# Attention over user histories: the softmax of a superblock two units earlier

## The reference

```python
cand = candidate_features @ Wi + bi                       # 512 x 64
hist = history_features @ Wi + bi                         # 512 x 200 x 64
hidden = relu((cand @ Wq)[:, None, :] + hist @ Wk)
scores = where(seq < history_length, hidden @ Wv, -1e9)   # 512 x 200
attn = softmax(scores, axis=1)
interest = einsum('bs,bse->be', attn, hist)
avg = sum(hist * mask, axis=1) / history_length
x = concatenate([interest, cand, avg], axis=1)
x = relu(bn(x @ W1 + b1)); x = relu(bn(x @ W2 + b2)); x = relu(bn(x @ W3 + b3))
return sigmoid(x @ Wo + bo)
```

## Time and profile before

| | |
|---|---|
| median of 3 runs | 216.58 us (216.19 to 216.93) |
| profiled execution, its own time | 215.18 us |
| its span, first to last instruction | 213.2 us |
| TensorE busy | 202.0 us, 95% |
| VectorE busy | 175.0 us, 82% |
| ScalarE busy | 103.6 us, 49% |
| GpSimd busy | 62.5 us, 29% |
| granted TensorE clock, mean | 0.989 |

### The profile page before, as it was taken

The page is one execution under the profiler, slowest core; times in us unless marked ns, Lnnn a source line. Parts: engine busy times, 40 slices in busy tenths (PEclk is TensorE's granted clock), DMA queues, the critical chain, the costliest instruction groups (busy, mean ns, idle before and its releaser), DMA issues.

```text
span 213.2 us, 6305 instructions
## 1 busy us (share of the span) xinstructions
PE 202.0 (95%) x2123; PEld 81.7 (38%) x2123; DVE 175.0 (82%) x1087; ACT 103.6 (49%) x302; POOL 62.5 (29%) x112
## 2 busy tenths in 40 slices
PE   7999999999999999999999999999999998996583
PEld 3433324343434334343434343434434343433321
DVE  1458464989989898989898998989798989989990
ACT  2045365636365553636463636556364646265423
POOL 7903041231506060504223150606051320504000
PEclk9999999999999999999999999999999999999995
DMA  6999999797969797988979797879798890000000
GB/s 188 408 425 415 413 411 363 237 323 242 329 241 334 236 324 246 307 291 293 311 241 329 235 313 270 313 223 311 263 315 298 252 340 29 3 0 3 5 0 0
DMA packets 10225, 53.72 MB, mean 252 GB/s; under 512 B 1105, under 2 KB 2001, under 8 KB 10194
## 3 DMA queue, kind: packets, MB, share of 16 engines
q1 hardware_dynamic: 9906, 52.95, 70.1%
q10 hardware_dynamic: 288, 0.37, 0.6%
HBM read 53.32 MB, written 0.00 MB: 250 GB/s over the span
## 4 chain that ended last, share of the span: by engine, by line
PE 85%; DVE 9%; issue 3%; ACT 1%; POOL 1%; POOLq 0%; DVEq 0%; ACTq 0%
PE hist_ps L397 42%; PE key_ps L412 23%; PE score_ps L423 11%; DVE scratch L553 5%; PE attn_ps L441 5%; PE score_ps L367 3%; DVE kept L540 2%; DVE attended L553 1%; ACT result L335 0%; POOLq L61 0%; PE attn_ps L480 0%; PE attn_ps L379 0%; POOL rest L265 0%; DVE scores L562 0%; DVE average L573 0%
## 5 line engine op out<-in xcount | busy, mean ns | idle before, releaser
L307 ACT ACTIVATE hidden<-key_ps,query 128x200 f32<-128x200 f32 x252 | 87.2, 429 | 88.5 <-PE key_ps L412 88.5
L540 DVE SCALAR_TENSOR_TENSOR kept<-item,lens,hist_ps 128x200 f32<-128x200 f32 x256 | 93.5, 415 | 11.5 <-PE hist_ps L397 11.5
L397 PE MATMUL hist_ps<-history,params 128*64 128x400 f32 x512 | 100.5, 512 | 0.7 <-DVE kept L540 0.7
L553 DVE CUSTOM_DVE_ANT_0 scratch<-attn_ps,kept 128x200 f32<-128x200 f32 x236 | 71.9, 359 | 16.0 <-PE attn_ps L441 16.0
L412 PE MATMUL key_ps<-kept,params 64*64 64x400 f32 x504 | 57.1, 521 | 0.6 <-DVE kept L540 0.2
L397 PEld LDWEIGHTS hist_ps<-history,params 128*64 128x64 f32 x512 | 30.6, 136 | 40.7 <-issue 26.9
L260 POOL TENSOR_SCALAR attn<-weights,inv_sum 128x200 f32<-128x200 f32 x15 | 6.5, 434 | 118.3 <-DVE inv_sum L568 118.3
L412 PEld LDWEIGHTS key_ps<-kept,params 64*64 64x64 f32 x504 | 13.5, 131 | 35.7 <-issue 27.0
L423 PE MATMUL score_ps<-hidden,wv_rows 128*32 128x200 f32 x512 | 25.0, 336 | 0.1
L441 PEld LDWEIGHTS attn_ps<-parts,spread 64*64 64x64 bf16 x472 | 14.8, 107 | 26.4 <-issue 16.5
L441 PE MATMUL attn_ps<-parts,spread 64*64 64x200 bf16 x472 | 21.1, 247 | 3.4 <-DVE parts L640 2.2
(11 more groups left out here) (70 smaller groups left out, 59.4 us busy)
## 6 DMA issues: line engine op xcount, KB each, us to landing
history<-history_dram SPq DMA_DIRECT2D x63, 800.0 KB, 4.9
history<-history_dram SPq DMA_DIRECT2D x2, 400.0 KB, 4.9
candT<-candidates_dram SPq DMA_DIRECT2D x1, 256.0 KB, 5.6
params<-parameters_dram SPq DMA_DIRECT2D x1, 248.5 KB, 12.4
params<-parameters_dram ACTq DMA_DIRECT2D x1, 226.5 KB, 2.6
lens_raw<-lengths_dram ACTq DMA_DIRECT2D x1, 136.0 KB, 4.0
probability<-result SPq DMA_DIRECT2D x1, 2.0 KB
```

The lines of the kernel that those rows point to most:

```text
L307: act.activation(hidden[:, g % HID_SLOTS, v, :], banks[:, v, at * SEQ:(at + 1) * SEQ], ACT.Relu, bias=query[:, 2 * g + v:2 * g + v + 1]).t ...
L397: product = pe.matmul(hist_ps[64 * h:64 * h + 64, g % 2, 0:QCOLS], param("wi"), history[:, slot, h, 2 * at:2 * at + 2, :].rearrange("f p s ...
L540: dve.scalar_tensor_tensor(out=kept[:, g % KEPT_SLOTS, u, :], in0=item[:, :], scalar=pair_len[:, col:col + 1], in1=hist_ps[:, g % 2, u * S ...
L553: dve.tensor_tensor_reduce(scratch[:, at, v, :], banks[:, at, v * SEQ:(v + 1) * SEQ], kept[:, q % KEPT_SLOTS, v, :], 1.0, 0.0, ALU.mult, A ...
```

## The change

`DELAY` goes from 9 to 7. The maximum of a superblock moves into the unit of its score (4j + 5, behind that unit's masked sums), the exponential ahead of the relus of unit 4j + 4 (those whose keys follow the score on TensorE), the reciprocal to the start of unit 4j + 6. The boundary of the MLP's two parts moves from unit 56 to unit 58, and with it the mean of the first part from unit 58 to unit 60. Behind the loop seven units are left for nine; the last score is made in two halves, the first ahead of the keys of unit 63, the second after two spreads; there are six warm-up matmuls for three, and the first two MLP stages come ahead of them. The last split on VectorE has four steps for five: the first two are fused into one for part a, and the rest is made by one instruction from weights, reciprocal and part a. The sums of unit 59 no longer stand between its steps.

```diff
-DELAY = 9
+DELAY = 7
 SCORE_AT = SB_UNITS + 1
-MAX_AT = SCORE_AT + 1
-TAIL_WARMUPS = 3
+TAIL_WARMUPS = 6
-PART_UNITS = UNITS - 8
+PART_UNITS = UNITS - 6
...
             for unit in range(UNITS):
-                j, at = divmod(unit + 1 - MAX_AT, SB_UNITS)
-                relu(unit)
+                j, at = divmod(unit + 1 - SCORE_AT, SB_UNITS)
                 if at == 0 and j >= 0:
                     exponent(j)
+                relu(unit)
             exponent(LAST)
...
-            def score(j):
-                pe.wait_ge(relu_done, 2 * SB_QUADS * (j + 1))
+            def score(j, steps=range(SB_UNITS)):
+                pe.wait_ge(relu_done, 2 * SB_QUADS * j + UNIT_PAIRS * steps.stop)
 
                 wait(pe, max_ready, j - 1)
-                for k in range(4):
+                for k in steps:
                     for c in range(4):
...
-                product.then_inc(scored, 1)
+                if steps.stop == SB_UNITS:
+                    product.then_inc(scored, 1)
...
             first = UNITS - DELAY
+            score(LAST, range(0, 2))
             keys(UNITS - 1)
             spread_attn(first)
             spread_attn(first + 1)
+            score(LAST, range(2, SB_UNITS))
             spread_attn(first + 2)
+            mlp_stage(0, 0)
+            mlp_stage(0, 1)
 
             pe.wait_ge(max_ready, LAST)
             for _ in range(TAIL_WARMUPS):
                 keep_busy((LAST + 1) % 2)
-            score(LAST)
             spread_attn(first + 3)
             spread_attn(first + 4)
-            mlp_stage(0, 0)
-            mlp_stage(0, 1)
+            mlp_stage(0, 2)
             spread_attn(first + 5)
+            mlp_stage(0, 3)
             spread_attn(first + 6)
-            mlp_stage(0, 2)
-            spread_attn(first + 7)
-            mlp_stage(0, 3)
-            spread_attn(first + 8)
             mlp_stage(1, 0)
...
             for unit in range(UNITS):
-                masked_sum(2 * unit)
-                j, at = divmod(unit - MAX_AT - 1, SB_UNITS)
+                j, at = divmod(unit - SCORE_AT - 1, SB_UNITS)
                 if at == 0 and j >= 0:
                     invert(j)
+                masked_sum(2 * unit)
                 masked_sum(2 * unit + 1)
-                j, at = divmod(unit - MAX_AT, SB_UNITS)
+                j, at = divmod(unit - SCORE_AT, SB_UNITS)
                 if at == 0 and j >= 0:
                     maximum(j)
...
             attended_sum(first)
-            attended_sum(first + 1)
             store_interest(0)
             mean(1)
+            attended_sum(first + 1)
+            maximum(LAST)
             attended_sum(first + 2)
-            maximum(LAST)
-            attended_sum(first + 3)
             invert(LAST)
...
-            dve.tensor_scalar(attn[:, :], weights[:, bank, :], inverse, None, ALU.mult).then_inc(split_steps, 1)
             dve.tensor_scalar(part_a[:, :], weights[:, bank, :], inverse, param("keep1"),
                               ALU.mult, ALU.mult).then_inc(split_steps, 1)
-            attended_sum(first + 4, (0,))
+            dve.wait_ge(split_steps, done + 1)
+            dve.scalar_tensor_tensor(out=rest[:, :], in0=weights[:, bank, :], scalar=inverse, in1=part_a[:, :],
+                                     op0=ALU.mult, op1=ALU.subtract).then_inc(split_steps, 1)
             dve.wait_ge(split_steps, done + 2)
-            dve.tensor_tensor(rest[:, :], attn[:, :], part_a[:, :], ALU.subtract).then_inc(split_steps, 1)
-            attended_sum(first + 4, (1,))
+            dve.tensor_scalar(part_b[:, :], rest[:, :], param("keep2"), None, ALU.mult).then_inc(split_steps, 1)
             dve.wait_ge(split_steps, done + 3)
-            dve.tensor_scalar(part_b[:, :], rest[:, :], param("keep2"), None, ALU.mult).then_inc(split_steps, 1)
-            attended_sum(first + 4, (2,))
-            dve.wait_ge(split_steps, done + 4)
             dve.wait_ge(attn_spread, SB_UNITS * (LAST - 1))
             dve.tensor_tensor(parts[:, bank, :], rest[:, :], part_b[:, :], ALU.subtract).then_inc(parts_ready, 1)
-            attended_sum(first + 4, (3,))
-            for unit in range(first + 5, UNITS):
+            for unit in range(first + 3, UNITS):
                 attended_sum(unit)
             store_interest(1)
```

## The result

The changed kernel takes **211.69 us** in the median of 6 runs (211.09 to 212.40), the kernel before, in the same session, 216.8 (216.19 to 217.76): ratio 0.977, interval 0.9744 to 0.9795. That is 5.1 us less; 2.3 less and at best 213.3 were forecast. The sign held; the gain is about twice what the sum gave, and the time lies outside the range.

A forecast was written before the change was run, and what follows sets the result against it. TensorE was taken to bound the loop (85% of the chain), VectorE's sums and the last parts the end. Terms 0.1 - 0.84 + 0.75 - 0.3 - 2.05 = -2.3 us, from 216.58 to 214.3; range 213.3 to 216.1.

The forecast's parts named there:

- late relus: ScalarE, score's unit: relus behind the exponential start 0.05 us late in each of fifteen superblocks, +0.75 us (0.15 to 2.25).
- From there the work is the same: sixteen sums, interest, four layers: Behind the spread of the last parts: remaining work unchanged, so no gain or loss beyond the -2.05 us before it.
- I put the difference on the median: Whole kernel: profiled execution 215.18 us, median 216.58; the 1.40 between them was carried over to the changed kernel's time.
- The three added fillers fall into TensorE's wait: End of kernel: added warm-up matmuls fall into TensorE's 2.17 us wait for the last parts' spread; no time effect was counted.
- the late bound: ScalarE, score's unit: if nothing overlaps the exponential's accumulator read, relus are 0.15 us late per superblock, 2.25 in all.
- the rivals that need 0.20 or more: Loop, ScalarE: relu's wait of 0.20 us per superblock, 216.5, chance 0.09; exponential binding from 0.21, 218.7, chance 0.08.
- VectorE's lateness: Loop, fourth unit: late masked sum stalls TensorE's projection 0.07 us; moving the maximum removes it twelve times, -0.84 us.
- The mean in unit 60: Before superblock 14's maximum: exponential, relus and keys 0.5 us late once, against 0.79 saved at the old place, -0.3 us.
- The end: From the loop's last spread to the last parts' spread: reciprocal 1.36 us earlier, shorter split, -2.05 us in all.
- the rival by which the end gains 0.7: Behind the loop: another late input leaves half the reciprocal's gain and none in the split; whole -1.0, 215.6 us, chance 0.13.
- The parts: Loop, GpSimd: parts ready before the first spread needing them, cover 0.28 us after release, cost nothing.
- The rival with late parts: Loop, GpSimd: parts 0.5 us later miss their spread, 0.22 lost per superblock, whole +1.0, 217.6 us, chance 0.03.

The follow-up runs named there:

- moved_gap: Kernel before with maximum, exponential and reciprocal moved, delay 9 and old end kept, plus ten warm-up matmuls in the wait for the last parts: median 213.84 us.
- after_more: Kernel after with twelve warm-up matmuls for six in the wait for the last parts and one more on each side of spread 62: median 211.68 us.
- moved_only: Kernel before with only maximum, exponential and reciprocal moved, delay 9 and the old end kept: median 216.1 us, ratio 0.9918.

## Why the prediction was wrong in size

Stages of the profiles, us, from the timelines; "usual before" is the second profile of the kernel before:

| stage | usual before | after | difference | forecast |
|---|---|---|---|---|
| start to first score | 21.72 | 21.30 | -0.42 | 0 |
| first superblock | 11.36 | 11.47 | +0.11 | +0.1 |
| second score to the loop's last spread | 158.50 | 157.36 | -1.14 | -0.44 |
| to the spread of the last parts | 10.48 | 8.65 | -1.83 | -2.05 |
| to the output's DMA | 10.94 | 9.34 | -1.60 | 0 |

The sum is -4.9, and the spans are 214.6 and 209.7. (The loop's forecast is -0.84, -0.3 and 14 of the 15 late relus, +0.70.)

**The step that failed** is "From there the work is the same: sixteen sums, interest, four layers", together with "I put the difference on the median". The work is the same, but in most executions of the kernel before it ran at half the clock, from about 2 us after the 2.17 us wait. The profile on which the sum was made is of the rare executions in which the clock falls only at 208.5. The 1.40 by which it lay under the median were this: against the second profile it had 1.84 less behind the last parts and 0.47 more at the start. Being a loss of one stage, they were not to be carried over to the changed kernel, whose wait is partly filled (1.46 left, 2.62 without fillers) and which loses less of its clock. "The three added fillers fall into TensorE's wait" was costed at nothing, and that was the gain: the kernel after has all six of its fillers directly ahead of that wait, and without them it loses 2.3, with as long a stretch behind the last parts as the usual run before (10.91 and 10.94). Which part of it three of them give, no run tells. Filling the wait of the kernel before gives 1.7, and filling it further after gives nothing that the times show. The sign of the gap was in view: the earlier trace rows show the wait, and the profiled time lay below all three runs shown.

Of the 2.5 us by which the table's 4.9 exceeds its forecast of 2.4, 1.6 are this stage and 0.7 the loop; the end has 0.2 less than forecast, and 0.4 is the start, by chance. The sign itself rests on the loop and the end, by the mechanisms that were forecast.

**The late relus** were sized 0.05 and cost about 0.02: superblocks of 11.50 to 11.52 (one of 11.62) against 11.49. Their start of 2.51 after the score, for 2.47, would be 0.04, but the keys behind them start 4.02 after the score for 4.00: the prediction let a late relu reach TensorE in full, and here half of it does. The relu does start while the accumulator is read, 104.23 + 0.19 - 104.32 = 0.10 before its end, so the late bound and the rivals that need 0.20 or more fell. Costing 0.03 less than sized, over 14 superblocks they are 0.4 of the loop's -0.70 beyond the forecast. The Trainium skill, "ScalarE: Activation LUTs", section "What ACT_TABLE_LOAD costs", has 93 ns of overlap for back-to-back ACTIVATEs; here the read has it too.

**VectorE's lateness**, 0.07 twelve times: right (though the profile of before has, beside 0.28 and 0.35, one of 0.55 and one of 1.06, the latter in the superblock with the mean): after the change the projections follow their spread by 0.28 to 0.31, but for one by 0.41, in the superblock of 11.62. moved_gap confirms the net gain of the moves, 0.9.

**The mean in unit 60**: forecast 0.5 late, once. Timeline after:

```profile
184.54 0.36 DVE L561 CUSTOM_DVE_ANT_0 scores<-score_ps,mask_bias 128x200 f32<-128x200 f32 x1
...
185.40 1.36 ACT L306 ACTIVATE hidden<-key_ps,query 128x200 f32<-128x200 f32 x4
...
186.91 0.90 PE L411 MATMUL key_ps<-kept,params 64*64 64x400 f32 x8 [0.36 <-ACT hidden L306]
```

The relus start 185.40 - 182.49 = 2.91 after the score, 0.40 later than in other superblocks, and the keys wait 0.36: right, and 0.1 better. With the relus' 0.4 and this, about 0.2 of the loop's difference is left, as much as executions of one kernel differ there (157.36 and 157.57 for after and after_more). The traces show a place for it: the usual run before has one superblock of 11.76 among those of 11.56, in which a projection follows its spread by 0.55. The profile of the kernel after has none such, that of after_more has one (11.76 among 11.50), so the change is not what removed it; what causes it was not traced.

**The end**: -1.83 for -2.05. Reciprocal to spread 1.94 for 1.88, with the fused rest 0.43 for 0.42; the other 0.16 lies ahead of the reciprocal, 6.71 from the loop's last spread for 6.55. So the rival by which the end gains 0.7 fell. **The parts** were sized right: ready 0.45 before their spread, 0.29 with the release of 0.16 taken off, for 0.28. From reciprocal (105.59) to the end of the parts it is 3.01, as in the earlier trace rows. The rival with late parts fell.

**Open**: the start differs by execution (21.30 to 22.19 in the profiles of both kernels and their variants), so its -0.42 is no part of the change. Against runs of the kernel before at 0.989, 214.97, the change is worth 3.3; by stages behind the start it is 2.6 with the profile of the kernel after and 3.1 with that of after_more. Why the clock falls early in most runs and late in some is open.

## What to carry to other kernels

Before a sum is made on a profile, hold its time and mean granted clock against those of the runs: where they differ, find the stage that has the difference, because a change there may win or lose it whole. A wait of TensorE ahead of a last, serial stretch can cost, beside its own length, the clock of what follows, as here, so a few useless matmuls in it can pay (1.7 us here). And a gain ahead of such a wait shows in the times only between runs of like clock: against the usual run, moved_only gained 1.0 in its profile up to the last parts and lost as much behind them. Where a step moves ahead of others in a queue, look at what its own input now holds up: with the reciprocal early and the exponential late, each superblock lost 0.35.

## What the runs showed of the hardware

The same program with the same wait of 2.2 us had a mean granted clock of 0.989 in 10 of 63 runs and of 0.969 to 0.977 in 53, which took 1.5 us more. In one profile of each kind TensorE fell from the 2.4 GHz to the 1.2 GHz level 6 us and 2 us after the wait. In one execution it fell after a wait of only 1.15 us (clock 0.51, score 2.44 for 1.56) and was back at 1.00 some 4 us later. An ACTIVATE starts 0.10 us before the accumulator read ahead of it ends. The fused multiply and subtract of 128x200, first operand in fp32 and second in bfloat16, took 0.43, the plain subtraction of the same shapes 0.37.
